# Attention of a fused network: query and key projections made once per batch in dense rows, staged through DRAM and loaded head by head; row maxima taken two heads ahead

## The reference, cut to what matters

```python
qkv = einsum('oc,bchw->bohw', w_qkv, x)          # x is group-normalised before
q, k, v = split(qkv, 3, axis=1)                  # each: 8 heads x 48 channels x 1024 positions
att = softmax(einsum('bhxd,bhyd->bhxy', q * 48**-0.5, k))
out = einsum('bhxy,bhyd->bhxd', att, v)
out = einsum('oc,bchw->bohw', w_proj, out) + b_proj    # plus the input, as a residual
```

## Time and profile before

| | |
|---|---|
| time, median of 3 runs | 4934.52 us (4933.33 to 4936.31) |
| time of the profiled execution | 4934.93 us |
| its span | 4933.3 us, granted clock 0.96 |
| PE busy | 4420.9 us (90%) |
| DVE busy | 3114.3 us (63%) |
| ACT busy | 2416.2 us (49%) |
| POOL busy | 1192.6 us (24%) |

### The profile page before, as it was taken

How to read it: one execution, slowest core, us unless ns; L and a number is a source line. 1 busy time by engine, 2 the same in 40 slices (tenths; PEclk the granted TensorE clock), 3 DMA queues, 4 the chain that set the end, 5 groups by cost and what they waited for, 6 DMA issues and landing times. The chain is left out here.

```text
span 4933.3 us, 48107 instructions
## 1 busy us (share of the span) xinstructions
PE 4420.9 (90%) x14579; PEld 2648.6 (54%) x14579; DVE 3114.3 (63%) x3139; ACT 2416.2 (49%) x3705; POOL 1192.6 (24%) x920
## 2 busy tenths in 40 slices
PE   5999999999999999848999999499399999999999
PEld 4666666666666767623444443388234444444444
DVE  4656666666666666656555554333487788678767
ACT  3757675858585757532222222112154455445544
POOL 2656565555555656400000000111000000000000
PEclk8999999999999999979999999799699999999999
DMA  2010101010101111020011000324200000000000
GB/s 49 21 51 20 50 20 50 20 50 21 47 24 38 33 38 33 28 100 13 39 54 49 39 26 26 103 82 129 109 26 38 38 0 38 38 38 0 38 38 13
DMA packets 62414, 205.55 MB, mean 42 GB/s; under 512 B 32016, under 2 KB 33680, under 8 KB 52496
## 3 DMA queue, kind: packets, MB, share of 16 engines
q1 hardware_dynamic: 56944, 191.90, 11.4%
q0 software_dynamic: 3840, 11.01, 1.0%
q10 hardware_dynamic: 1440, 0.16, 0.0%
HBM read 133.95 MB, written 51.27 MB: 38 GB/s over the span
## 5 line engine op out<-in xcount | busy, mean ns | idle before, releaser
L456 POOL TENSOR_TENSOR probs_lo<-probs,probs_hi 128x512 fp32r<-128x512 f32 x840 | 1116.3, 1351 | 900.7 <-ACT probs L511 889.5
L510 ACT ACTIVATE probs_hi<-s_psum 128x512 fp32r<-128x512 f32 x1024 | 619.0, 605 | 302.7 <-PE s_psum L734 282.9
L2237 PE MATMUL psum<-mixes,conv_t 128*128 128x512 f32 x1728 | 751.1, 592 | 0.0
L581 DVE TENSOR_REDUCE maxima<-m_psum 128x1 fp32r<-128x1024 f32 x520 | 632.1, 1223 | 90.6 <-PE m_psum L712 73.6
L511 ACT ACTIVATE probs<-s_psum 128x512 f32<-128x512 f32 x1024 | 617.9, 603 | 0.0
L2237 PEld LDWEIGHTS psum<-mixes,conv_t 128*128 128x128 f32 x1728 | 327.5, 190 | 409.8 <-issue 409.8
L733 PE MATMUL s_psum<-q_all,k_hi 128*128 128x512 f32 x1026 | 433.6, 423 | 102.7 <-ACT probs L511 102.7
L749 PE MATMUL o_psum<-probs_lo,v 128*112 128x512 f32 x1024 | 410.1, 400 | 17.8 <-DVE probs_lo L652 17.8
L744 PE MATMUL o_psum<-probs_hi,v 128*112 128x512 f32 x1024 | 407.0, 397 | 0.0
L734 PE MATMUL s_psum<-q_all,k_lo 128*128 128x512 f32 x1026 | 404.9, 395 | 0.0
L712 PE MATMUL m_psum<-k_hi,q_all 128*128 128x512 f32 x1040 | 335.9, 405 | 19.8 <-DVE maxima L581 16.2
(11 more groups left out here) (312 smaller groups left out, 7105.2 us busy)
## 6 DMA issues: line engine op xcount, KB each, us to landing
xin<-in_x SPq DMA_DIRECT2D x18, 1536.0 KB, 6.7
xin<-x SPq DMA_DIRECT2D x17, 1536.0 KB, 6.9
xres<-x SPq DMA_DIRECT2D x16, 1536.0 KB, 7.2
k_hi<-k_hi SPq DMA_DIRECT2D x66, 256.0 KB, 3.3
xb<-x SPq DMA_DIRECT2D x4, 4096.0 KB, 16.0
inv_wide<-inv_row SPq DMA_DIRECT2D x64, 192.0 KB, 2.8
x<-xin SPq DMA_DIRECT2D x8, 1536.0 KB, 5.4
x<-xres SPq DMA_DIRECT2D x8, 1536.0 KB, 5.0
```

Source lines behind the costliest of these rows:

```text
L456: pool.tensor_tensor(probs_lo[:, u % RING, :], probs[:, u % RING, :], as_f32(probs_hi[:, u % RING, :]), ALU.subtract).then_inc(pool_low.ne ...
L510: nc.scalar.activation(probs_hi[:, u % RING, :], s_psum[:, u % 2, :], ACT.Exp, scale=SCALE)
L581: nc.vector.tensor_reduce(maxima[:, MAX_ROW + tile:MAX_ROW + tile + 1], slot(tile % 2), AX.X, ALU.max, negate=True).then_inc(rows_max.next ...
L2237: ins = nc.tensor.matmul(bank, conv_w[:, t, down, factor, m * P:(m + 1) * P], mixes[:, factor, t, down:down + S, :].rearrange("p a b -> p ...
```

## The change

- The projections of query and key use dense weights (384 columns, no padding). A batch has 12 pieces (`PIECES`), each 128 output channels by 512 positions: 9 matmuls. A piece's high part goes to `stage_hi` (ACT), its low part to `stage_lo` (DVE), and SP writes both to DRAM (`stage`, two transfers of 256 KB). In a pass, head 0 has the last two pieces of its own batch, heads 3 to 7 two each of the next batch. A piece's matmuls go in three chunks of three, in units 1, 3, 5 or 9, 11, 13; ACT splits in units 6 and 14, DVE in 7 and 15.
- SP loads each head from DRAM into its slot (`load_head`, five transfers of 48 rows x 1024), three heads ahead, behind `move_sums` of the head before.
- Row scores are two heads ahead (`AHEAD`), one tile in each even unit, in one slot (banks 0 and 1 of `m_psum`). A tile holds every eighth query (`tile::KEYS`), so that the column of maxima runs through the row of queries in order, and SP moves `maxima` straight into `q_all`. The turning matmuls and ACT's copy are gone.
- The group norm of the next batch moves to heads 0 (statistics), 1 and 2. `VECTOR_LOWS` becomes units 4, 9, 14, in heads 1 and 2 units 5 and 11 (22 a pass; 23 before). The residual's load moves from head 7 to head 4; the next batch's input is loaded at the start of a pass.
- Before the loop: ten pieces, three heads loaded, row scores of two heads; POOL fills `k_hi` and `q_all` with zeros besides what it filled.

```diff
-    ROW_UNITS = (2, 3, 4, 5, 6, 7, 8, 9)
-    ROWS_AT, TURN_AT, K_AT, Q_AT = ROW_UNITS[0], 11, 12, 14
-    GN_AT = HEADS - 5
-    VECTOR_LOWS = [(h, n) for h in range(HEADS) for n in (0, 12, 14) if h > 0 or n > 0]
+    PIECES = 4 * CT
+    LATE = 2
+    EARLY = PIECES - LATE
+    PIECE_AT = {}
+    for n in range(PIECES):
+        head, part = ((0, n) if n < LATE else (3 + (n - LATE) // 2, (n - LATE) % 2))
+        PIECE_AT[head, part] = ((n + EARLY) % PIECES, int(n >= LATE))
+    CHUNK_UNITS = ((1, 3, 5), (9, 11, 13))
+    SPLIT_UNITS = (6, 14)
+    AHEAD = 2
+    VECTOR_LOWS = [(h, n) for h in range(HEADS) for n in ((5, 11) if h in (1, 2) else (4, 9, 14))]
+    MEASURE_AT = [(0, 11), (0, 12), (0, 13), (0, 14), (0, 15), (1, 0)]
+    MOMENTS_AT, GROUPS_AT, VARIANCE_AT, RSTD_AT = (1, 1), (1, 3), (1, 4), (1, 5)
+    NORMALISE_AT = [(1, 7), (1, 9), (1, 11)]
+    HIGH_AT = [(1, 12), (1, 15), (2, 4)]
+    LOW_AT = [(1, 13), (2, 2), (2, 7)]
...
+            def load_head(g, i):                                        # SP
+                slot, b, first = g % SLOTS, g // HEADS, g % HEADS * HEAD
+                last = 4 * ((first + HEAD - 1) // P) + 2
+                for parity in range(2):
+                    sp.wait_ge(staged[parity], piece_total(last + parity, b, i, 32) + 32)
+                for tile, at, name in ((k_hi, 0, ("k", "hi")), (k_hi, 64, ("k", "hi")), (k_lo, 0, ("k", "lo")),
+                                       (q_all, 0, ("q", "hi")), (q_all, 64, ("q", "lo"))):
+                    sp.dma_start(as_f32(tile[at:at + HEAD, slot, :]), staged_rows(name, b, i, first, first + HEAD)).then_inc(head_loaded[g % 2], 16)
+            def stage(p, ahead, i):
+                m, name, half = p // 4, ("k", "q")[p // 2 % 2], p % 2
+                sp.wait_ge(qk_low.sem, qk_low.at(piece(p, ahead, i), i))
+                for part, tile in (("hi", stage_hi), ("lo", stage_lo)):
+                    target = staged_rows((name, part), ahead, i, m * P, (m + 1) * P)[:, cols_of(half)]
+                    sp.dma_start(target, as_f32(tile[:, half, :])).then_inc(staged[half], 16)
+            def place_max(g, i):
+                sp.wait_ge(rows_max.sem, rows_max.at(row(g, KEYS - 1, i), i))
+                sp.dma_start(as_f32(q_all[HEAD:HEAD + 1, g % SLOTS, :]).rearrange("a (p j) -> a p j", j=KEYS),
+                             as_f32(maxima[:, g % 2, :])).then_inc(max_placed[g % 2], 16)
...
             with sp.Fori(0, B) as i:
                 for h in range(HEADS):
+                    if h == 0:
+                        sp.wait_ge(stored, i * 16 + 16)
+                        sp.dma_start(xin[:, :], whole(bass.ds((i + 1) % B, 1))).then_inc(x_loaded, 16)
+                    else:
+                        move_sums(h - 1, i)
+                    load_head(h + 3, i)
                     if h > 0:
-                        move_sums(h - 1, i)
+                        move_inverse(h - 1, i)
                         widen(h - 1, i)
...
+                    for part in range(2):
+                        if (h, part) in PIECE_AT:
+                            stage(*PIECE_AT[h, part], i)
+                    place_max(h + AHEAD, i)
...
+            def split(p, ahead, i):                                     # ACT
+                act.wait_ge(qk_made.sem, qk_made.at(piece(p, ahead, i), i))
+                if i is not None or p >= 2:
+                    act.wait_ge(staged[p % 2], piece_total(p, ahead, i, 32))
+                nc.scalar.copy(stage_hi[:, p % 2, :], m_psum[:, 2 + p % 2, :]).then_inc(qk_high.next(), 1)
...
+            def row_max(g, tile, i):                                    # DVE
+                dve.wait_ge(rows_made.sem, rows_made.at(row(g, tile, i), i))
+                if tile == 0 and i is not None:
+                    dve.wait_ge(max_placed[g % 2], head_total(g - 2, i, 16))
+                nc.vector.tensor_reduce(maxima[:, g % 2, tile:tile + 1], m_psum[:, 0:2, :].rearrange("p a b -> p (a b)"),
+                                         AX.X, ALU.max, negate=True).then_inc(rows_max.next(), 1)
...
             def row_scores(g, tile, i):                                 # PE
                 if tile == 0:
+                    pe.wait_ge(head_loaded[g % 2], head_total(g, i, 80))
+                if i is not None or tile > 0 or g > 0:
+                    pe.wait_ge(rows_max.sem, rows_max.at(row(g, tile, i) - 1, i))
                 for half in range(2):
+                    ins = nc.tensor.matmul(m_psum[:, half, :], q_all[:, g % SLOTS, tile::KEYS],
+                                           k_hi[:, g % SLOTS, cols_of(half)], start=True, stop=True)
                 ins.then_inc(rows_made.next(), 1)
-            def turn_max(g, i):
-                pe.wait_ge(rows_max.sem, rows_max.at(nth(g, KEYS, i) + KEYS, i))
-                for tile in range(KEYS):
-                    ins = nc.tensor.matmul(m_psum[0:MAX_ROW + 1, tile // 4, (tile % 4) * P:(tile % 4 + 1) * P],
-                                           maxima[:, tile:tile + MAX_ROW + 1], ident_r[:, :], start=True, stop=True)
...
                 for u in range(N):
                     h, n = u // UNITS, u % UNITS
+                    if n % 2 == 0:
+                        row_scores(h + AHEAD, n // 2, i)
+                    for part in range(2):
+                        if (h, part) in PIECE_AT and n in CHUNK_UNITS[part]:
+                            project_qk(*PIECE_AT[h, part], CHUNK_UNITS[part].index(n), i)
+                    if (h, n) == GROUPS_AT:
+                        groups(i)
                     scores(u + LAG, i)
                     if u > 0:
                         weigh(u - 1, i)
```

More of the change, by code:

```diff
@@ L374, in attention_layer, with piece, piece_total, row @@
         filled = signal("filled")
[L375 to L384, removed]
+        def piece(p, ahead, i):
+            return p + 1 if i is None else p + 1 - EARLY + PIECES * ahead
+        def piece_total(p, ahead, i, per):
+            return (p // 2 + PIECES // 2 * ahead) * per + (0 if i is None else i * (PIECES // 2 * per))
+        def row(g, tile, i):
+            return g * KEYS + tile + 1 - (0 if i is None else KEYS * AHEAD)
+        def head_total(g, i, per):
+            return (g // 2 + 1) * per + (0 if i is None else i * (HEADS // 2 * per))
+        def cols_of(half):
+            return slice(half * HALF, (half + 1) * HALF)
         block = ctx.enter_context(nc.Block())
@@ L389, in _, with staged_rows @@
         def _(sp):
-            def place_max(g, i):
[L391 to L398, removed]
+            def staged_rows(name, b, i, first, last):
+                at = rows_dram[name][b:b + 1, first:last] if i is None else rows_dram[name][b:b + B][bass.ds(i, 1), first:last]
+                return at.rearrange("b p n -> (b p) n")
@@ L484, in copy_out @@
                     act.wait_ge(y_made.sem, y_made.at(0, i))
-                nc.scalar.copy(heads[row:row + 64, h // 2, half * HALF:(half + 1) * HALF], o_psum[0:64, half, :]).then_inc(o_copied.next(), 1)
+                nc.scalar.copy(heads[at:at + 64, h // 2, cols_of(half)], o_psum[0:64, half, :]).then_inc(o_copied.next(), 1)
             def keep_values(i):
@@ L495, in group_rstd @@
                 gn.scalar_rstd(act, act_step, i, gn_rstd)
-            nc.scalar.copy(ident_r[:, :], const["ident"]).then_inc(turned_ident.next(), 1)
             group_rstd(None)
-            for part in range(2):
-                split(0, part, None)
-            copy_max(0, None)
+            for p in range(EARLY):
+                split(p, 0, None)
             act.wait_ge(filled.sem, filled.at(ALL_FILLED))
@@ L615, in _ @@
                 split_low(t, None)
-            split(0, 0, None)
-            split(0, 1, None)
+            for p in range(8):
+                split(p, 0, None)
             for tile in range(KEYS):
                 row_max(0, tile, None)
+                if tile in (2, 5):
+                    split(8 + (tile == 5), 0, None)
             for tile in range(KEYS):
+                row_max(1, tile, None)
                 low_values(tile, None)
@@ new lines, in project_qk @@
+            def project_qk(p, ahead, t, i):
+                m, half = p // 4, p % 2
+                high, low = weights[("k", "q")[p // 2 % 2]]
+                if t == 0:
+                    if i is not None:
+                        last = piece(p, ahead, i) - 2
+                        pe.wait_ge(qk_low.sem, qk_low.at(last, i))
+                        if p == 0:
+                            pe.wait_ge(xn_ready.sem, xn_ready.at(CT, i))
+                            pe.wait_ge(gn_var.sem, gn_var.at(1, i))
+                    elif p >= 2:
+                        pe.wait_ge(qk_low.sem, qk_low.at(p - 1))
+                for k, (w, x) in enumerate(((high, xn_hi), (high, xn_lo), (low, xn_hi))):
+                    ins = nc.tensor.matmul(m_psum[:, 2 + p % 2, :], w[:, t, m * P:(m + 1) * P], x[:, t, cols_of(half)],
```

(9 more changed lines are left out.)

306 lines of the change are left out of this document (127 added, 179 removed).

## The result

The changed kernel takes 4790.86 us (median of 4 runs, 4790.4 to 4794.63) against 4933.93 (4 runs): a ratio of 0.9712, 95% interval 0.9695 to 0.9728. Forecast were 4810 and a range of 4725 to 4890.

What follows compares the result with a forecast made beforehand. PE's matmul list plus the places where PE stands was taken to set the pace. Terms summed to a pass of 229.7 us for 249.2: eight passes -156, start +31, so 4934.9 - 125 = 4810 us, range 4725 to 4890.

Steps and rivals of the forecast that it cites:

- PE's list: Loop over units: projections fall from 144 to 108 matmuls a pass, 36 x 0.2315 = 8.3 us less.
- Turn and copy: Chain PE, ACT, SP in each head: eight turns go, 5.3 us a pass, and 2 to 3 us lost a head end.
- Heads 1 and 2: Bare units meet the group norm on DVE: 26.3 and 22.0 us, 7.8 and 3.5 over PE's matmuls.
- The 2.5 us for the clock: Once a pass matmuls fall to the lower clock level after PE stood: 2.5 us kept, from 0 to 6.
- Low parts behind a maximum: Units 4 and 14: DVE's low part stands behind that unit's reduction, 0.65 x 6 = 3.9 us a pass.
- The end of a pass: First value matmul to next scores, 34.4 us, 35.5 with the last weighing: nothing of it changes.
- The start: Before the loop: fillings, ten pieces, head loads and maxima tiles move first scores to about 130 us; +31, bounds 18 and 50.
- Rival C: Row scores' strided weight loads double to 0.376 us: 18.5 us a pass, 4958 us in all; chance 0.05.
- A: The forecast itself: whole kernel 4810 us, own range 4780 to 4850; chance 0.53.
- B: DVE keeps up, no low part late, clock doesn't fall: pass 218, 4716 us in all; chance 0.20.
- D: DVE and POOL in each other's way in all heads: pass 239, 4884 us in all; chance 0.16.
- E: Head loads come late or staging stops ACT: 2 us a head, 16 a pass, 4938 us; chance 0.06.

## Why the prediction was right

**PE's list.** 0.2315 us for each of 36 matmuls fewer: 8.3 forecast; 32 fewer in the kernel before gave 6.9, 36 more in the changed one took 6.9, so 36 are worth 6.9 to 7.8. On the path in both.

**Turn and copy.** Forecast were 5.3 for the matmuls and the 2 to 3 us a head of waits for ACT. PE's wait for ACT fell by 11.2 us a pass; the short turn alone gave 7.3. The reading of the waits was too high: they were 12.7 us a pass before, 1.6 a head, and the trace doesn't put the rest of the 2 to 3 down to ACT.

**The pass added up.** 6.9 to 7.8 us go with the projections, 5.3 with the turns (the forecast's price) and 11.2 with waits for ACT. New are 2.7 of waits for DVE's low parts, 2.9 for the stride and 1.6 at the end of a pass. That leaves 16 to 17 of the 20.7 us; the rest isn't attributed.

**Heads 1 and 2.** 26.3 and 22.0 forecast, 28.1 and 21.9 measured. The mechanism stood: DVE's order between maxima. Sizes were off in head 1, by 1.8 together. The normalising steps took 1.75 to 1.90 us where I had charged 1.3, and the first high part 1.77 where I had 1.1. The 2.5 us for the clock stood apart in the sum; from 865.4 on ten matmuls take 0.43 us each and not 0.23, by my estimate about 2 us more, of which about 0.9 lies in head 1. So that term was good, and the clock is half of what head 1 has over 26.3. Units 0 to 6 took 12.2 for my 11.0, and yet the table loads were worth only 1.6 of my 2.8. The statistics in head 0 cost less than my 1.5: the first pass has head 0 at 155.05 - 132.69 = 22.4 us, and its 98 matmuls alone are 22.7.

**Low parts behind a maximum.** 3.9 forecast, 4.4 given back when they moved. It is seen in unit 14 of each head with pieces, with PE standing 0.5 to 0.6 us, where the count of nine matmuls put it; in unit 4 PE never waits.

**The end of a pass.** "Nothing of it changes" was wrong. From the first value matmul it took 34.4 us to the next scores; now it takes 36.0 to the next row scores, 1.6 more in each of the seven. Row scores begin in unit 0 in two banks from which DVE still reads the last output tiles, and PE waits 1.1 us for its residual (L682). With 229.7 forecast and 228.6 measured, other terms made up for it, head 0 above all (22.4 us where the sum had 22.7 + 1.5): in part luck.

**The start.** +31 forecast, +31.5 measured. So close a hit is luck, for the parts were less good than their sum: the stall of the staging buffers was there (ACT waits 12.3 us for one write), the fillings of POOL cost nothing in the end, since the shorter weight stage gave back all 7 us (DVE starts at 41.88, before at 42.12), and the tiles of maxima took 2.55 us each at the lower clock where I had 2.1.

**Rival C, strided weights,** had no term in the sum, and has one: 2.9 us a pass. The row that I read it from had 81 loads of another layer at 202 ns with neighbours 27 elements apart, and didn't carry over to neighbours 8 apart, which takes 323. What saved the forecast is that both loads of a tile mostly hide: the pair costs 0.49 us from start to start where it was 0.46. The rule in the Trainium skill ("SBUF — State Buffer", section "Door 1: The DMA port swizzle"), a penalty beyond four fp32 elements, agrees with 323 ns against 188 at a stride of eight fp32r elements; it gives no size, and at 27 fp32 elements show hardly any, 202 against 188. Two slips in the prediction change nothing: the 125 us are gone at 125/(8 x 128) = 0.122 us more a load, not 0.115, and "faster 0.89" is already A, B and D without a part of E.

**Missed.** The end of the layer: 6.9 us (6.6 between the two transfers on SP) because a useless load of 1536 KB is gone. The remaining 3.3 us of the 10.2 lie in layers whose code is the same. Over the kernels here that share this end these layers took 2827.9 to 2833.0 us, so 3.3 is within their spread; what sets the spread stays open.

**Rivals B, D, E.** B had the pass at 218. With spread norm steps and moved low parts the pass is 221.9, so 6.7 of the 10.6 us between the two were to be had, by another order. D: the median of DVE's low parts is 0.80 us, 0.69 before, and 4.9 us a pass is all that PE waits for them. E: no wait for a load in the loop, even with the loads nine us later.

## What to carry to other kernels

Count the matmuls in the list of the engine that sets the pace and price them at their distance from start to start, not at their recorded duration: taken away or added, a projection matmul was worth 0.19 to 0.22 us of its 0.23, in both kernels. Where a ring of one buffer ties that engine to another, look at what the other has queued between two of its releases; moving two low parts a head by one unit was worth 32 us, leaving out the logarithm with its table loads 6. When work moves to the start of a round, look at who still reads its buffers: here that cost 1.6 us a pass. A stop of PE can cost twice, when its clock falls beside it: ten matmuls at 0.43 for 0.23 us came with stops of 3.3 us. With the norm steps spread it fell once in the loop; with low parts moved as well it fell in seven of eight passes, so taking stops away doesn't by itself keep the clock up.

## What the runs showed of the hardware

- A weight load of 128x128 with neighbours eight fp32r elements (32 bytes) apart takes 323 ns, a contiguous one 188, and one with neighbours 27 fp32 elements apart 202. I had not expected the shorter stride to be the dearer one. The operands differ in type as well, which was not separated.
- Eight transfers of 128 single values take 5.0 us together to issue, 0.60 each in the median; one of 128 runs of eight values takes 0.49.
- DVE's normalising step of 128x1024 takes 1.75 to 1.90 us beside a busy POOL, 0.80 at least.
- Writes of 256 KB from SBUF to DRAM landed in 2.1 to 2.4 us, reads of 192 KB in 3.3 to 5.2, issued five at a time:

```profile
k_hi<-k_rows_hi SPq DMA_DIRECT2D x134, 192.0 KB, 3.3
k_rows_hi<-stage_hi SPq DMA_DIRECT2D x54, 256.0 KB, 2.2
...
q_all<-q_rows_lo SPq DMA_DIRECT2D x67, 192.0 KB, 5.2
```
